# A two-layer block on one core: the first layer taken chunk by chunk, and a new order ahead of its second recurrence

## What is computed

```python
# layer 0, first part: 16 heads of dk = 8
r, k, v = xr @ Wr, xk @ Wk, xv @ Wv
g = silu(xg @ Wg)
w = w0 + tanh(xw @ wA) @ wB;  decay = exp(-exp(w))
# scan over tokens
o = r . (S + u * kv);  S = decay * S + kv          # kv = k (outer) v
o = (o - mean) * rsqrt(var + 1e-5) * gn_w + gn_b   # per head (group norm)
x = x + (o * g) @ Wo
x = x + gelu(rms_norm(x) @ ffn_w1) @ ffn_w2
# layer 0, second part: top-1 routing to 8 experts
# layer 1, first part
xb, zb = x @ in_proj;  u = silu(conv4(xb));  proj = u @ x_proj
dt = softplus(dt_raw @ dt_proj + b);  a = -exp(A_log) * (0.5 + sigmoid(gate))
state = exp(dt * a) * state + dt * b_t * u_t       # 256 channels x 16 states, scan over tokens
y = sum(state * c_t) + D * u;  x = x + ga * ((y * silu(zb)) @ out_proj)
# layer 1, second part: top-8 of 16 experts and a shared one
```

## Time and profile before

| | |
|---|---|
| median of three runs | 684.94 us (684.94, 685.04, 679.49) |
| profiled execution | 678.64 us |
| its span, first to last instruction | 676.9 us |
| instructions | 6762 |
| mean granted TensorE clock | 0.932 |

### The profile page before, as it was taken

How to read it: one execution, slowest core, us unless ns; L and a number is a source line. 1 busy time by engine, 2 the same in 40 slices (tenths; PEclk the granted TensorE clock), 3 DMA queues, 4 the chain that set the end, 5 groups by cost and what they waited for, 6 DMA issues and landing times.

```text
span 676.9 us, 6762 instructions
## 1 busy us (share of the span) xinstructions
PE 573.5 (85%) x1896; PEld 318.3 (47%) x1896; DVE 530.1 (78%) x728; ACT 384.9 (57%) x662; POOL 395.2 (58%) x345
## 2 busy tenths in 40 slices
PE   6597674669989998978888777988878999999997
PEld 3133321226666952323333222323325777888885
DVE  0784998453677969669999999999999856766674
ACT  4566100658721337877886865675666466555553
POOL 0004888425200020348999999999978546666665
PEclk9699776869969999989998998998999999999999
DMA  8000000800011000100000000010100633434330
GB/s 312 22 1 1 0 0 1 330 1 1 1 63 62 1 1 0 46 1 0 0 0 24 23 24 24 24 35 2 48 0 6 193 99 93 136 115 145 111 109 17
DMA packets 14598, 35.11 MB, mean 52 GB/s; under 512 B 1952, under 2 KB 2240, under 8 KB 13952
## 3 DMA queue, kind: packets, MB, share of 16 engines
q1 hardware_dynamic: 14560, 34.67, 15.7%
HBM read 33.46 MB, written 1.20 MB: 51 GB/s over the span
## 4 chain that ended last, share of the span: by engine, by line
PE 33%; DVE 27%; POOL 17%; issue 15%; ACT 6%; DMA 1%; POOLq 0%; DVEq 0%; SPq 0%; ACTq 0%
DVE arena L1734 9%; POOL h_parts L1941 8%; POOL arena L1814 7%; PE ps L1002 7%; PE ps L654 6%; DVE arena L1500 4%; DVE arena L1709 4%; PE ps L937 4%; PE ps L784 2%; DVE ps L1484 2%; DVE ps L1661 1%; PE ps L801 1%; PE ps L881 1%; PE ps L722 1%; PE ps L725 1%
## 5 line engine op out<-in xcount | busy, mean ns | idle before, releaser
L1814 POOL TENSOR_TENSOR arena<-arena 128x512 f32<-128x512 f32 x184 | 228.1, 1272 | 34.4 <-DVE arena L1734 17.1
L1734 DVE TENSOR_TENSOR_SCAN arena<-ps,carry,arena 128x512 f32<-128x512 f32 x128 | 156.4, 1263 | 0.0
L937 PE MATMUL ps<-arena,core 128*128 128x512 f32 x256 | 127.5, 617 | 2.2 <-POOL arena L1814 1.8
L1361 ACT ACTIVATE ps<-arena,abase 128x512 f32<-128x512 f32 x128 | 88.1, 691 | 62.5 <-DVE arena L1734 61.7
L1941 POOL TENSOR_TENSOR h_parts<-arena,h_parts 128x512 fp32r<-128x512 f32 x68 | 88.0, 1295 | 60.6 <-ACT h_parts L1395 59.7
L1002 PE MATMUL ps<-x_parts,w_hi 128*128 128x512 f32 x272 | 99.9, 407 | 1.1 <-DVE arena L1709 0.7
L1709 DVE TENSOR_TENSOR arena<-ps,arena 128x1024 f32<-128x1024 f32 x64 | 76.8, 1200 | 8.3 <-PE ps L1042 8.2
L1802 DVE TENSOR_TENSOR ps<-ps,arena 128x512 f32<-128x512 f32 x64 | 44.6, 697 | 41.9 <-PE ps L1002 33.4
L1042 PE MATMUL ps<-bc,sel 96*128 96x512 bf16 x128 | 44.0, 388 | 37.1 <-ACT arena L1355 23.2
L1403 ACT ACTIVATE arena<-ps 128x512 f32<-128x512 f32 x68 | 40.6, 598 | 60.4 <-PE ps L1002 59.3
L937 PEld LDWEIGHTS ps<-arena,core 128*128 128x128 f32 x256 | 48.8, 195 | 43.8 <-issue 24.3
(11 more groups left out here) (235 smaller groups left out, 986.0 us busy)
## 6 DMA issues: line engine op xcount, KB each, us to landing
arena<-weight_rows SPq DMA_DIRECT2D x64, 256.0 KB, 3.3
arena<-in_wB SPq DMA_DIRECT2D x2, 2048.0 KB, 12.3
arena<-in_wD SPq DMA_DIRECT2D x8, 384.0 KB, 3.1
arena<-in_cstB SPq DMA_DIRECT2D x1, 1368.0 KB, 5.6
wC<-in_wC SPq DMA_DIRECT2D x1, 1040.0 KB, 11.5
x<-in_x SPq DMA_DIRECT2D x4, 256.0 KB, 4.2
arena<-slot_rows SPq DMA_DIRECT2D x4, 256.0 KB, 3.9
arena<-scale_rows SPq DMA_DIRECT2D x4, 256.0 KB, 3.7
```

What stands on the lines that cost most here:

```text
L937: mm(bank(c + 2 * (i % 2)), CORE_("eye"), PRC[:, (2 * q + c) % PR_RING, :], start=False, stop=(n == NS - 1)).then_inc(*done(f"y{n}_{c}", i))
L1361: A(bank(6 + c), ch(DTG[:, c, :], i), ACT.Exp, scale=ABASE[:, c * NS + n:c * NS + n + 1]).then_inc(*done(f"dec{n}_{c}", i))
L1734: nc.vector.tensor_tensor_scan(ST[:, k % ST_RING, :], bank(6 + c), DBU[:, (2 * q + c) % DBU_RING, :], CARRY[:, k:k + 1], ALU.mult, ALU.add ...
L1814: mul = lambda o, a, b: nc.gpsimd.tensor_tensor(o, a, b, ALU.mult)
```

## The change

**Start.** All four means of norm A precede the modulation, which is made per layer (mod0, mod1) into banks 4 and 5. DVE normalises two chunks, takes the first layer's modulation, then goes on; the other modulation steps follow the fourth. ACT takes sqB and the roots of norm B with the first root early; DVE threads xx between the norms. PE's sweeps are k, v, lora_a, r. ACT does tanh with the set of exp, so that one table load is in front of the sweeps and none between tanh and w_exp, then v_hi and r_copy by turns.

**First recurrence.** PE makes lora_b(0), then begins the spreads; lora_b(1 to 3) follow the first three. At columns 5 to 8 PE adds g and head_ruk of chunk 0 to 3 (banks 0 and 1), ACT g_silu, and DVE the bonus after the scans of columns 4 to 7. ACT loads the silu set at column 0, after the decay copy, and the set of log and exp after column 8. At columns 18 to 21 ACT makes g * gn_b into V and g * gn_w in place. At columns 31 and 33 PE takes group norm steps of chunks 0 to 2 (TAIL_PE).

**Group norm to feed-forward.** Chunk by chunk. The Newton step is folded: gn_scaled = -0.5 * centred * root, gn_err in PSUM, gn_norm = (err - 3) * scaled. gn_w and gn_b are in the gate: gn_gate multiplies by g * gn_w, and a second product wo_b with Wo on g * gn_b accumulates with wo. Norm C works in PSUM banks (VAR_BANK), and f_x_hi is a second DVE operation beside normC.

**Ahead of the second recurrence.** modE and the scaling of xb1 go from DVE to ACT. z of chunk 0 follows the gates. dt is taken in three parts of fp32r side by side in 24 rows (dt_hi on ACT, dt_parts on DVE; the weights dt_w_hi, dt_w), one pass. bc_mid and bc_lo of chunks 2 and 3 go into turns 1, 2 and 5, 7, the products Du of chunk 0 into turns 0 and 1. At turn 0 the decays precede the copy of c.

The core of the diff:

```diff
+GATE_COLUMN, BONUS_COLUMN = 5, 4
+GN_COLUMN = 2 * DK + 2
+VAR_BANK = (2, 0, 3, 1)
+TAIL_PE = {NR - 1: [("gn_centred", 0)], NR + 1: [("gn_centred", 1), ("gn_var", 0), ("gn_var", 1), ("gn_centred", 2)]}
...
-            sweep("r", W("Wr"), M0, 1, ["mix_r", "lnA"])
-            sweep("k", W("Wk"), M1, 0, ["mix_k", "lnB"])
-            sweep("v", W("Wv"), M2, 1, ["mix_v", "r_copy"])
-            sweep("lora_a", W("wA"), M0, 0, ["mix_w", "k_copy"], rows=LORA)
-            sweep("g", W("Wg"), M1, 1, ["mix_g", "v_copy"])
-            sweep("lora_b", W("wB", slice(0, LORA)), TA, 0, ["lora_tanh"], parts=LORA)
-            sweep("head_ruk", C("head_sum"), XX, 1, ["ruk", "g_silu"])
-
-
-            pe.wait_ge(*upto("bonus", NCH - 1))
-            pe.wait_ge(*upto("w_exp", NCH - 1))
...
+            sweep("k", W("Wk"), M0, 1, ["mix_k", "lnA"])
+            sweep("v", W("Wv"), M1, 0, ["mix_v", "lnB"])
+            sweep("lora_a", W("wA"), M2, 1, ["mix_w", "k_copy"], rows=LORA)
+            sweep("r", W("Wr"), M0, 0, ["mix_r", "v_copy"])
+
+            def lora_b(i):
+                pe.wait_ge(*upto("lora_tanh", i))
+                pe.wait_ge(*upto("r_copy", i))
+                mm(half(0, i), W("wB", slice(0, LORA)), ch(TA, i)[0:LORA], start=True, stop=True).then_inc(*done("lora_b", i))
+
+            def gate_and_bonus(i):
+
+                pe.wait_ge(*upto("mix_g", i))
+                pe.wait_ge(*(upto("g_silu", i - 1) if i else upto("w_exp", 0)))
+                mm(bank(0), W("Wg"), ch(G, i), start=True, stop=True).then_inc(*done("g", i))
+                pe.wait_ge(*upto("ruk", i))
+                pe.wait_ge(*(upto("bonus", i - 1) if i else upto("w_exp", 1)))
+                mm(bank(1), C("head_sum"), ch(M2, i), start=True, stop=True).then_inc(*done("head_ruk", i))
+
+            def gn_centred(i):
+                pe.wait_ge(*upto("o", i))
+                pe.wait_ge(*column("scan{}", NR - NCH + i))
+                mm(half(1, i), C("gn_centre"), ch(O, i), start=True, stop=True).then_inc(*done("gn_centred", i))
+
+            def gn_var(i):
+                pe.wait_ge(*upto("gn_sq", i))
+                pe.wait_ge(*(column("scan{}", (2 * DK - 1) if i == 0 else NR - 1) if i % 2 == 0 else upto("o", LAST - 1 + i // 2)))
+                mm(bank(VAR_BANK[i]), C("gn_mean"), ch(T1, i), start=True, stop=True).then_inc(*done("gn_var", i))
+
+            def wo_b(i):
+
+                pe.wait_ge(*upto("gn_b_gate", i))
+                pe.wait_ge(*upto("gn_scaled", i))
+                mm(half(1, i), W("Wo"), ch(V, i), start=True, stop=False).then_inc(*done("wo_b", i))
+
+            def wo(i):
+                pe.wait_ge(*upto("gn_gate", i))
+                mm(half(1, i), W("Wo"), ch(O, i), start=False, stop=True).then_inc(*done("wo", i))
+
+            def ms_c(i):
+                pe.wait_ge(*upto("sqC", i))
+                pe.wait_ge(*upto("gn_norm", i))
+                mm(bank(VAR_BANK[i]), CORE_("mean"), ch(T2, i), start=True, stop=True).then_inc(*done("msC", i))
+
+            tail = {"gn_centred": gn_centred, "gn_var": gn_var}
...
+                    if q < LAST:
+                        lora_b(q + 1)
+                    if 0 <= q - GATE_COLUMN < NCH:
+                        gate_and_bonus(q - GATE_COLUMN)
...
-            pe.wait_ge(*upto("scan7", NCH - 1))
-            sweep("gn_centred", C("gn_centre"), O, 1, ["o"])
-            pe.wait_ge(*upto("o", NCH - 1))
-            sweep("gn_var", C("gn_mean"), T1, 0, ["gn_sq"])
-            sweep("wo", W("Wo"), O, 1, ["gn_gate"])
-            sweep("msC", CORE_("mean"), T2, 0, ["sqC", "gn_err"])
-            pe.wait_ge(*upto("lnC", NCH - 1))
+                for name, i in TAIL_PE.get(q, ()):
+                    tail[name](i)
+
+            gn_var(2)
+            gn_centred(3)
+            wo_b(0)
+            gn_var(3)
+            wo(0)
+            wo_b(1)
+            wo(1)
+            ms_c(0)
+            wo_b(2)
+            wo(2)
+            wo_b(3)
+            ms_c(1)
+            wo(3)
+            ms_c(2)
+            ms_c(3)
...
-            def z(i):
-                in_proj("z", DI * P, i, ("u0", "u1"))
...
+            def z(c):
+                a = wc_at["in"][0] + (DI + c) * P
+                pe.wait_ge(*upto(f"gate{c}_tanh", 0))
+                mm(half(c, 0), wC[:, a:a + P], ch(HC, 0), start=True, stop=True).then_inc(*done(f"z{c}", 0))
 
             def dt(i):
-                a = wc_at["dtp"][0]
-                pe.wait_ge(*upto("dt_raw_copy", i))
-                for c, w in enumerate(([], ["bc_r1"]) if i else (["gate0_tanh"], ["gate1_tanh"])):
-                    for name in w:
-                        pe.wait_ge(*upto(name, i))
-                    mm(half(c, i), wC[BC3:BC3 + DTR, a + c * P:a + (c + 1) * P], ch(DRAW, i)[BC3:BC3 + DTR],
-                       start=True, stop=True).then_inc(*done(f"dt{c}", i))
+                pe.wait_ge(*upto("dt_parts", i))
+                for c in range(DI):
+                    if i == 0:
+                        pe.wait_ge(*upto(f"z{c}_silu", 0))
+                    mm(half(c, i), DT_W[:, c * P:(c + 1) * P], ch(DT_X, i), start=True, stop=True).then_inc(*done(f"dt{c}", i))
...
-            for c in range(DI):
-                d_u(c, 0)
...
+            def gn_gates(i):
+
+                act.wait_ge(*upto("g_silu", i))
+                act.wait_ge(*upto("bonus", i))
+                act.wait_ge(*upto("v_lo", i))
+                A(ch(V, i), ch(G, i), ACT.Copy, scale=col("gn_b")).then_inc(*done("gn_b_gate", i))
+                act.wait_ge(*upto("gn_b_gate", i))
+                A(ch(G, i), ch(G, i), ACT.Copy, scale=col("gn_w")).then_inc(*done("gn_w_gate", i))
...
+            v_hi(0)
+            v_hi(1)
+            r_copy(0)
+            v_hi(2)
+            r_copy(1)
+            v_hi(3)
+            r_copy(2)
+            r_copy(3)
...
+                if q == 0:
+                    nc.scalar.preload_act_table_set("silu_and_others")
...
+                if 0 <= q - GATE_COLUMN < NCH:
+                    act.wait_ge(*upto("g", q - GATE_COLUMN))
+                    A(ch(G, q - GATE_COLUMN), bank(0), ACT.Silu).then_inc(*done("g_silu", q - GATE_COLUMN))
+                if 0 <= q - GN_COLUMN < NCH:
+                    gn_gates(q - GN_COLUMN)
+                if q == GATE_COLUMN + NCH - 1:
+                    nc.scalar.preload_act_table_set("natural_log_exp_and_others")
...
+            def gn_rsqrt(i):
+                square_of("gn_sq", half(1, i), T1, ["gn_centred"], i)
                 act.wait_ge(*upto("gn_var", i))
-                A(ch(T1, i), half(0, i), ACT.Ln, bias=col("eps5")).then_inc(*done("gn_ln", i))
+                A(ch(T1, i), bank(VAR_BANK[i]), ACT.Ln, bias=col("eps5")).then_inc(*done("gn_ln", i))
                 act.wait_ge(*upto("gn_ln", i))
                 A(ch(T1, i), ch(T1, i), ACT.Exp, scale=-0.5).then_inc(*done("gn_rs", i))
                 act.wait_ge(*upto("gn_rs", i))
                 A(ch(T3, i), ch(T1, i), ACT.Square).then_inc(*done("gn_rs2", i))
-                if i:
...
+            sq_c(0)
+            rsqrt_c(0)
+            sq_c(1)
+            rsqrt_c(1)
+            sq_c(2)
+            sq_c(3)
+            rsqrt_c(2)
+            rsqrt_c(3)
...
+            def gn_scaled(i):
+                dve.wait_ge(*upto("gn_rs", i))
+                stt(ch(O, i), half(1, i), -0.5, ch(T1, i), ALU.mult, ALU.mult).then_inc(*done("gn_scaled", i))
+
+            def gn_norm(i):
+
+                b = bank(VAR_BANK[i])
                 dve.wait_ge(*upto("gn_rs2", i))
-                stt(ch(T3, i), half(0, i), EPS_GN, ch(T3, i), ALU.add, ALU.mult).then_inc(*done("gn_err", i))
+                stt(b, b, EPS_GN, ch(T3, i), ALU.add, ALU.mult).then_inc(*done("gn_err", i))
                 dve.wait_ge(*upto("gn_err", i))
-                ts(ch(T3, i), ch(T3, i), -0.5, 1.5, ALU.mult, ALU.add).then_inc(*done("gn_half", i))
-                dve.wait_ge(*upto("gn_half", i))
-                tt(ch(T1, i), ch(T1, i), ch(T3, i), ALU.mult).then_inc(*done("gn_rsqrt", i))
-                dve.wait_ge(*upto("gn_rsqrt", i))
-                tt(ch(O, i), half(1, i), ch(T1, i), ALU.mult).then_inc(*done("gn_norm", i))
-            for i in range(NCH):
+                stt(ch(O, i), b, -3.0, ch(O, i), ALU.add, ALU.mult).then_inc(*done("gn_norm", i))
+
+            def x1(i):
                 dve.wait_ge(*upto("wo", i))
                 tt(ch(HLN, i), half(1, i), ch(HLN, i), ALU.add).then_inc(*done("x1", i))
-            for i in range(NCH):
+
+            def norm_c(i):
+                b = bank(VAR_BANK[i])
                 dve.wait_ge(*upto("rsC", i))
-                stt(ch(M0, i), ch(HLN, i), col("ln2_w"), ch(T2, i), ALU.mult, ALU.mult).then_inc(*done("normC", i))
+                stt(ch(M0, i), ch(HLN, i), col("ln2_w"), b, ALU.mult, ALU.mult).then_inc(*done("normC", i))
+                stt(ch(f_x_parts[:, 0, :], i), ch(HLN, i), col("ln2_w"), b, ALU.mult, ALU.mult).then_inc(*done("f_x_hi", i))
+
```

(35 more changed lines are left out.)

## The result

| | before | after |
|---|---|---|
| median of the runs | 682.27 us (4 runs: 684.94, 685.04, 679.49, 679.59) | 659.34 us (4 runs, 658.89 to 659.92) |
| profiled execution | 678.64 us | 658.89 us |
| its span | 676.9 us | 657.1 us |
| mean granted TensorE clock | 0.932 | 0.953 |

The ratio is 0.967, with a 95% interval of 0.963 to 0.971: 3.3% faster. The forecast, 657 us between 646 and 670, holds the time. Its two large terms came out as worked out. One term taken as nothing, the turns of the second recurrence, did not, and most of the experiments are about it.

A forecast was written before the change was run, and what follows sets the result against it. No engine is full over the whole span (TensorE 85%, VectorE 78%); three stages are loose. Profiled 678.64 us less 10, 14 and 0 gives 654.6; about half of the median's 6.3 excess added: 657 us, range 646 to 670.

The forecast's parts named there:

- two large terms: Start and first recurrence together 10 us gained (7 to 12); group norm to feed-forward 14 us more (3 to 18).
- the turns of the second recurrence: Pieces of bc and Du moved into these turns fit POOL's idle time: cost nothing, or 2.3 us if that were gone.
- Start: Up to the first scan: mixes 4.2 us earlier, POOL's first product on kv_aside at 53.8, 10.5 us earlier.
- The bound of 0.7 each: Start: ruk products beside a running POOL product take up to 0.7 us longer each, 2.9 for four; 0.4 counted.
- First recurrence: It ends at 108.1 in place of 118.2; start and recurrence together gain 10 us, between 7 and 12.
- the held-up gates: First recurrence: gate and head products waiting in PE's queue lose 0.4 us; as a rival 6.6 us, 664, chance 0.11.
- Group norm to feed-forward: From 108.1 to the first gelu at 132: 24 us where 37.6 were, 14 gained, between 3 and 18.
- The rival of a half-clock tail: PE stays at half clock from group norm to feed-forward, gaining 3 us there: 669 us, chance 0.14.
- Ahead of the second recurrence: Stage before the second recurrence's first scan: walk gave 0.8 us gained, 0 taken, between a loss and a gain of 4.
- the rival that ends slower: Second recurrence: with Du gone PE idles, turns stay at half clock, 2.5 us lost each; 14 give 692; chance 0.05.
- The sign that was given: From the second recurrence's first scan to the end, the length stays 381 us as before.
- the 6.3: How far the earlier median, 684.94 us, lay above the profiled execution, 678.64; about half was added to the sum.

The follow-up runs named there:

- table_late: The changed kernel with the silu table load moved from column 0 to just ahead of the first g_silu in column 5: 659.39 us, ratio 0.967.
- tail_old: The changed kernel with group norm to feed-forward as in the kernel before: 673.09 us, ratio 0.988.
- f_old: The changed kernel with its whole stage ahead of the second recurrence as in the kernel before: 655.64 us, ratio 0.962.
- f_old_table: f_old with the silu table load moved to column 5: 658.9 us, ratio 0.967.
- best: The changed kernel with chunk 0's Du back ahead of the second recurrence, silu load in column 5, three unread products, 48 bytes ahead of wC: 656.46 us.
- one_du: f_old_table with only Du0 ahead of the second recurrence and Du1 behind the first b and c spreads: 658.0 us, ratio 0.966.
- f_shift: f_old with 144 bytes left empty in each partition ahead of wC: 657.15 us, ratio 0.965.

## Why the prediction was right, and where it was not

**Start.** Forecast: mixes at 27.2, first spread 44.5, first product on kv_aside 53.8. Measured: 26.11, 45.32, 54.39. What was to set the time did: ACT's eight decay operations, the table load, the copy, then POOL. The Trainium skill's 1.38 us drain after a table load (ScalarE: Activation LUTs, What ACT_TABLE_LOAD costs) is not to be seen here either: the load at 52.42 ends at 53.70 and the copy starts at 53.72. DVE waited 0.88 us for the product, not 2, since its own first scan came at 50.07 and not at 47.3. That is in the main ruk beside a running POOL product: 1.48 us each (5.92 for four) where it took 0.68 in the kernel before. The bound of 0.7 each was a little small; the choice to count most of it as hidden was right, and table_late shows what it hides: without the load DVE's own queue sets the fourth scan, so the start can't gain much more than 1 us there. The mark itself agrees in part by luck: from the first mix to the product on kv_aside the forecast had 26.6 us and the trace has 28.3, and the first mix, which moves by up to 2.9 us between profiles, came 1.1 us earlier here than forecast.

**First recurrence.** Forecast 10 us by its end, with 0.4 for the held-up gates. The last scan is 9.89 earlier and DVE waits for PE in none of the columns 5 to 9. The size is right; of its make-up, 5.35 lie ahead of the first mix (4.2 forecast) and 4.5 behind it (5.8 forecast).

**Group norm to feed-forward.** Forecast 24 us from 108.1 to a gelu at 132, with 2 for the clock. Measured: 108.2 to 131.75. The clock was 0.93. One product, gn_var of chunk 1, ran at the lower level behind a gap in PE of 2.59 us, at 108.24 for 2.07 us, and gn_centred of chunk 2 behind it took 1.71 in part at it; the others took 1.02 to 1.12. The rival of a half-clock tail did not happen, and tail_old gives the term by itself, 13.5 to 13.75 for the 14.

**Ahead of the second recurrence.** Forecast 0, between a loss of 4 and a gain of 4. Measured: 0.26 lost, and 0.2 by f_old. Right in size, and the reason given holds: ACT took what DVE gave (43.46 us busy in the 57.9 us up to the first scan, where it had 38.30 in 57.7).

**The turns: the step that failed.** It said of the moved pieces "nothing, or 2.3 if that were gone". That looked at POOL's and ACT's free time and was right of them: bc_mid and bc_lo cost nothing, the distance to the kernel before is the same from turn 3 to turn 20. What the sum priced at nothing was taking Du away ahead of the recurrence. The text does name it, as the rival that ends slower: PE idles, the clock falls, 2.5 us per turn. That rival had the mechanism and the wrong length. The clock did fall, and came back within two turns, with PE busy for 4.00 of the four us before 276: 2.5 us in all, not per turn. The argument that dismissed the rival ("at half clock PE would never idle, and there it rose before") says why it stays small; it does not make it zero. A term of 2 to 3 us belonged in the sum. The sign that was given, 381 us from the first scan to the end, came out at 385.3.

**The experts and the turns before them.** No term; 0.6 us lost in the later turns and 1.2 in the experts. The last three turns and the experts' first ones (0.4 and 0.3) go with a fall of the clock at 490.4, some 0.7 with the products of 397 ns, whose cause is open.

**From the sum to the median.** The sum gave 654.6 for the profiled execution, measured 658.89: 4.3 us too little, just what is lost behind the first gelu. Then 2.4 us were added (half of the 6.3 would be 3.2) since the median before lay above its profiled run. That was not needed: the changed kernel's median lies 0.45 above its profiled run. The forecast of 657 is only 2.3 off because these two errors have opposite signs, which is luck.

## What to carry to other kernels

Taking work off PE ahead of a stage in which it is needed at once can cost more than the work: ask what clock the stage will start with, and price the first products at the lower level. When a piece is taken out of a change that wins, measure the pieces: here the new stage costs 2.5 us by what the runs show, a tenth of what the rest gains, and the whole still looks good. Where a time comes in two groups, look at the granted clock of the runs before comparing medians.

## What the runs showed of the hardware

- TensorE's clock can fall while the engine has work. In f_old_table it was 0.50 from 257.4 to 273.4 with PE busy for 4.00 of every 4 us, through products of 8 rows (8 x 128 by 8 x 512) and then Du; in f_old, with the same queue, it fell near 261, some 5.7 us later against the first gelu. In best it fell at 266 behind products of 24 and of 128 rows with PE busy for 3.34 of 4 us. The Trainium skill, TensorE: Matmul & The Clock Gate, What's actually happening, has activity release the throttle; busy time alone did not do that here. Whether it is the few rows of these products was not tried.
- A fall of the clock at the end of a stage is paid in the next one. In one_du four instructions took 2.91 us for 1.88 and eight small ones 1.73 for 0.96 at the end of the turns, and the experts' third silu came 1.68 us late, though the clock was back at 1.00 by then.
- The same fp32 products with wD have a median of 393 ns in one build and 397 in another, with the same clock of 1.00 and no gap on PE, and with nothing but 144 empty bytes added ahead in SBUF (f_old, f_shift) they went from one to the other. From the 31st turn of the experts to the last it is 0.74 us.
- With nothing changed ahead of it, the first mix came at 25.5 to 28.4 us. Distances between marks told more than marks.
